# Two cross-attention and expert layers on one core: routing steps of the first attention moved, merged heads put in another PSUM bank

## What is computed

```
x = x + attention0(layernorm(x), ctx, ctx)    # 16 heads of 8 channels, rotary, 256 x 256 scores a head
x = x + experts0(layernorm(x))                # 64 experts, each token's best 8, softmax weights
x = x + attention1(layernorm(x), ctx, ctx)    # one head
x = x + experts1(layernorm(x))                # 16 experts, each token's best 4
```

## Time and profile before

| | us |
|---|---|
| median of three runs | 686.94 (686.65 to 692.87) |
| profiled execution, its own time | 690.62 |
| its span in the profile | 688.9 |
| TensorE busy in the span | 482.5 (70%) |
| VectorE busy | 384.4 (56%) |
| ScalarE busy | 221.6 (32%) |
| GpSimd busy | 349.4 (51%) |

### The profile page before, as it was taken

How to read it: one execution, slowest core, us unless ns; L and a number is a source line. 1 busy time by engine, 2 the same in 40 slices (tenths; PEclk the granted TensorE clock), 3 DMA queues, 4 the chain that set the end, 5 groups by cost and what they waited for, 6 DMA issues and landing times.

```text
span 688.9 us, 12080 instructions
## 1 busy us (share of the span) xinstructions
PE 482.5 (70%) x3519; PEld 368.4 (53%) x3519; DVE 384.4 (56%) x1235; ACT 221.6 (32%) x578; POOL 349.4 (51%) x476
## 2 busy tenths in 40 slices
PE   0741898888898430699989994157764499999960
PEld 0630344444443210688877783145553499999950
DVE  8981576788786460154444442689955044444426
ACT  0451065555667310333323331134431122222210
POOL 9394221115556673256545537014444867777730
PEclk9985599888899655799999998597765599999985
DMA  5089989746588697789999723961111799999927
GB/s 184 4 203 244 341 291 298 218 94 155 166 238 279 208 402 285 229 270 313 347 298 309 244 95 106 353 273 55 70 69 61 258 388 360 349 353 361 375 100 276
DMA packets 82915, 163.95 MB, mean 238 GB/s; under 512 B 13070, under 2 KB 58142, under 8 KB 81072
## 3 DMA queue, kind: packets, MB, share of 16 engines
q1 hardware_dynamic: 56832, 106.20, 46.3%
q0 software_dynamic: 13968, 32.29, 12.7%
q10 hardware_dynamic: 12064, 24.84, 12.4%
HBM read 104.94 MB, written 66.78 MB: 249 GB/s over the span
## 4 chain that ended last, share of the span: by engine, by line
PE 32%; DMA 13%; DVE 9%; issue 2%; POOL 2%; ACT 1%; SPq 1%; POOLq 0%; DVEq 0%
PE sc_ps L1790 11%; DMA hd_side<-held 6%; PE hd_ps_up L1246 6%; PE sc_ps L1772 5%; DMA rows<-hd_side_out,hd_side_target 3%; PE hd_ps_out L1252 2%; DMA sc_rows<-rows 2%; PE hd_ps_x L1224 2%; PE sc_ps L1780 1%; DVE sc_rows L1879 1%; PE sc_ps L1740 1%; POOL rows L1393 1%; PE sc_ps L1728 1%; DVE sc_n_stats L1473 1%; DMA listed<-sc_empty,sc_index 1%
## 5 line engine op out<-in xcount | busy, mean ns | idle before, releaser
L1021 DVE TENSOR_REDUCE at_top<-at_ps_top 128x2 f32<-128x512 f32 x128 | 83.2, 685 | 46.4 <-PE at_ps_top L926 45.6
L1393 POOL DMA_INDIRECT rows<-hd_out,hd_rows x64 | 62.2, 972 | 59.3 <-DVE hd_out L1344 36.9
L1093 ACT ACTIVATE at_prob<-at_ps_score 128x512 f32<-128x512 f32 x128 | 72.6, 594 | 51.2 <-PE at_ps_score L944 50.6
L926 PE MATMUL at_ps_top<-e_arena 96*128 96x256 bf16 x256 | 57.6, 315 | 37.2 <-PEq L107 21.9
L1246 PE MATMUL hd_ps_up<-hd_x_turned,e_arena 128*128 128x160 f32 x512 | 82.7, 305 | 0.0
L1790 PEld LDWEIGHTS sc_ps<-sc_t_turned,e_w 128*112 128x112 f32 x672 | 80.6, 180 | 2.6
L1790 PE MATMUL sc_ps<-sc_t_turned,e_w 128*112 128x128 f32 x672 | 82.0, 276 | 0.0
L1246 PEld LDWEIGHTS hd_ps_up<-hd_x_turned,e_arena 128*128 128x128 f32 x512 | 76.1, 192 | 8.7 <-issue 6.2
L682 POOL DMA_INDIRECT held<-e_extended,e_address x64 | 62.4, 975 | 28.4 <-issue 17.7
L682 POOL DMA_INDIRECT listed<-e_extended,e_address x32 | 33.6, 1049 | 69.0 <-DVE e_address L674 61.5
L1381 DVE TENSOR_TENSOR hd_inner<-hd_silu,hd_ps_up 128x160 f32<-128x160 f32 x64 | 20.5, 321 | 81.8 <-ACT hd_silu L1331 81.8
(11 more groups left out here) (266 smaller groups left out, 911.6 us busy)
## 6 DMA issues: line engine op xcount, KB each, us to landing
e_w<-in_weights SPq DMA_DIRECT2D x42, 704.0 KB, 6.0
e_arena<-in_weights SPq DMA_DIRECT2D x52, 384.0 KB, 11.4
held<-e_empty ACTq DMA_DIRECT2D x16, 960.0 KB, 7.2
hd_rows<-held SPq DMA_DIRECT2D x15, 768.0 KB, 10.5
sc_rows<-rows SPq DMA_DIRECT2D x8, 1024.0 KB, 13.8
sc_tile_rows<-listed SPq DMA_DIRECT2D x42, 144.0 KB
parts<-op_parts SPq DMA_DIRECT2D x8, 576.0 KB, 6.7
e_arena<-in_weights ACTq DMA_DIRECT2D x12, 384.0 KB, 4.0
```

Source lines behind the costliest of these rows:

```text
L926: last = nc.tensor.matmul(ps_top[at % TOPS][:, half, :], q_in[n][0:TOP, columns(at, half)], k_in[n][0:TOP, columns(at)], start=True, stop= ...
L1021: nc.vector.reduce_max(top[:, 2 * h:2 * h + 2], ps_top[at % TOPS][:], AX_X).then_inc(top_found, 1)
L1093: nc.scalar.activation(prob[at % RING][:], ps_score[at % SCORES][:], ACT.Exp, scale=scale).then_inc(prob_ready, 1)
L1393: nc.gpsimd.indirect_dma_start(rows_out, to, out_ap, None, bounds_check=TOKENS * LAYER0.chosen - 1, oob_is_err=False).then_inc(semaphore, 16)
```

## The change

It renumbers the routing steps, gives each batch's eight scatters steps of their own, splits the table of the last two batches, moves the turn, the copy and the placing of the cut maxima one step later each, and puts the merged heads into the second half of the bank of `ps_rows`, with the waits that go with it.

```
-    LOAD, SHARE = 26, 34
-    AMID = dict(load=LOAD, share=SHARE, merge=37, add=38, scale=39, norm=42, turn=46, keep=47, score=51, choose=52, expo=55, rank=55,
-                places=57, targets=59, weights=62, scatter=62)
-    LAST_BUT_TWO = dict(AMID, turn=45, keep=46, score=49, choose=49, expo=50, targets=50, rank=50, places=51, weights=51, scatter=53)
-    LAST_TWO = dict(load=LOAD, share=SHARE, merge=35, add=36, scale=37, norm=37, turn=39, keep=39, score=41, choose=41, expo=42, targets=42,
-                    rank=43, places=43, weights=43, scatter=46)
+    AMID = dict(load=26, share=34, merge=37, add=38, scale=39, norm=42, turn=45, keep=46, score=49, choose=50, expo=52, rank=53,
+                places=54, targets=55, weights=57)
+    LAST_BUT_TWO = dict(AMID, score=48, choose=48, expo=49, rank=49, places=50, targets=50, weights=51)
+    LAST_BUT_ONE = dict(load=26, share=31, merge=32, add=33, scale=34, norm=34, turn=36, keep=36, score=38, choose=38, expo=39, targets=39,
+                        rank=40, places=40, weights=40)
+    LAST = dict(load=26, share=34, merge=35, add=36, scale=37, norm=37, turn=39, keep=39, score=41, choose=41, expo=42, targets=42,
+                rank=43, places=43, weights=43)
+    SCATTERS = (57, 58, 60, 61, 62, 64, 65, 66)
+    LAST_SCATTERS = tuple(range(51, 59))
 
     def __init__(self):
-        of_batch = [self.AMID] * (B - 3) + [self.LAST_BUT_TWO] + [self.LAST_TWO] * 2
+        of_batch = [self.AMID] * (B - 3) + [self.LAST_BUT_TWO, self.LAST_BUT_ONE, self.LAST]
...
+            for k, offset in enumerate(self.SCATTERS if b < B - 3 else self.LAST_SCATTERS):
+                self.scatters.setdefault(b * H + offset, []).append((b, k))
...
-            first = b * H + offsets["scatter"]
-            apart = H // 2 if first < B * H - H - 4 else LAYER0.chosen // 2
-            for k in range(LAYER0.chosen):
-                self.scatters.setdefault(first + k % 4 + k // 4 * apart, []).append((b, k))
...
-        ps_rows = s.psum("ps_rows", [P, P])
+        ps_rows_merged = s.psum("ps_rows_merged", [P, 2 * D])
+        ps_rows, ps_merged = ps_rows_merged[:, 0:P], ps_rows_merged[:, D:]
         ps_merge = s.psum("ps_merge", [P, 2 * D])
-        ps_merged = ps_merge[:, 0:D]
...
-                hh, late = divmod(at + LEAD - 5, HALF)
+                hh, late = divmod(at + LEAD - 6, HALF)
                 if late == HALF - 1 and 0 <= hh < HALVES:
                     place(hh)
...
                 if hh >= 1:
                     pe.wait_ge(rows_kept, hh)
+                if hh == 1:
+                    pe.wait_ge(lift_known, 1)
+                if hh >= 6 and hh % 2 == 0:
+                    pe.wait_ge(x_ready, hh // 2 - 2)
...
                 pe.wait_ge(inputs.loaded, 48)
+                pe.wait_ge(rows_kept, 1)
...
             def merge(b):
-                if b >= B - 2:
-                    pe.wait_ge(routing.rank_read, b)
-                elif b >= 1:
-                    pe.wait_ge(routing.logits_read, b)
-                else:
-                    pe.wait_ge(lift_known, 1)
+                pe.wait_ge(rows_kept, min(2 * b + 6, HALVES))
+                if b >= 1:
+                    pe.wait_ge(x_ready, b)
                 pe.wait_ge(divided, b + 1)
...
-                hh, late = divmod(at + LEAD - 4, HALF)
+                hh, late = divmod(at + LEAD - 5, HALF)
                 if late == HALF - 1 and 0 <= hh < HALVES:
                     turn_tops(hh)
...
-                    if b + 1 < B - 2:
-                        pe.wait_ge(x_ready, b + 2)
                     routing.pe_rank(pe, b)
...
-                hh, late = divmod(at + LEAD - 5, HALF)
+                hh, late = divmod(at + LEAD - 6, HALF)
                 if late == HALF - 1 and 0 <= hh < HALVES:
                     keep_rows(hh)
```

More of the change, by code:

```diff
@@ L752 @@
 class RoutingSteps:
-    LOAD, SHARE = 26, 34
-    AMID = dict(load=LOAD, share=SHARE, merge=37, add=38, scale=39, norm=42, turn=46, keep=47, score=51, choose=52, expo=55, rank=55,
-                places=57, targets=59, weights=62, scatter=62)
-    LAST_BUT_TWO = dict(AMID, turn=45, keep=46, score=49, choose=49, expo=50, targets=50, rank=50, places=51, weights=51, scatter=53)
-    LAST_TWO = dict(load=LOAD, share=SHARE, merge=35, add=36, scale=37, norm=37, turn=39, keep=39, score=41, choose=41, expo=42, targets=42,
-                    rank=43, places=43, weights=43, scatter=46)
+    AMID = dict(load=26, share=34, merge=37, add=38, scale=39, norm=42, turn=45, keep=46, score=49, choose=50, expo=52, rank=53,
[7 more added lines that the diff above has]
+    LAST_SCATTERS = tuple(range(51, 59))
     def __init__(self):
-        of_batch = [self.AMID] * (B - 3) + [self.LAST_BUT_TWO] + [self.LAST_TWO] * 2
-        self.batch = {}
+        of_batch = [self.AMID] * (B - 3) + [self.LAST_BUT_TWO, self.LAST_BUT_ONE, self.LAST]
+        self.batch, self.scatters = {}, {}
         for b, offsets in enumerate(of_batch):
@@ L768, in __init__ @@
                 self.batch[stage, b * H + offset] = b
+            for k, offset in enumerate(self.SCATTERS if b < B - 3 else self.LAST_SCATTERS):
+                self.scatters.setdefault(b * H + offset, []).append((b, k))
         self.end = max(at for _, at in self.batch) + 1
-        self.scatters = {}
-        for b, offsets in enumerate(of_batch):
-            first = b * H + offsets["scatter"]
-            apart = H // 2 if first < B * H - H - 4 else LAYER0.chosen // 2
-            for k in range(LAYER0.chosen):
-                self.scatters.setdefault(first + k % 4 + k // 4 * apart, []).append((b, k))
         self.first_scatter = min(self.scatters)
```

## The result

The changed kernel takes 707.55 us (median of 4, 706.42 to 712.17) where the kernel before takes 686.88 in the same session: ratio 1.0292, 95% interval 1.022 to 1.0364. It is slower by 20.7 us; forecast was 9. The profiled execution took 708.05 us, span 706.3.

What follows compares the result with a forecast made beforehand. The prediction took POOL's end of the first layer's routing, its last 32 scatters, as the bound. Heads 9.1 us later less 0.2 in the tail gave about +9 on the median 686.94: 696.0 us, range 684 to 702.

Steps and rivals of the forecast that it cites:

- The stretch at full clock: Steps from 50, 66, 82, 98: share and choose in one DVE block, 2.4 us per stretch, 2.2 in the last.
- the moved routing score: Routing score's four PE matmuls move from step 16b+35 to 16b+33, where PE is full: 0.5 us per stretch.
- The credit for old half clock: Three earlier stretches: 0.5 us off each, since old half clock there might not be lost twice.
- The first 50 steps: New PSUM bank's waits taken as 0, also at step 40; bounds -0.5 to +0.5 us per batch.
- The clock behind step 50: Batches 0 to 3's closer steps: heads 9.1 us later, without added half clock in the main forecast.
- clock rival: Longer PE stalls behind each share add some 10 us of half clock, 4 us lost, 700 us; chance 0.15.
- The cut behind two scatters: Last stretch, batch 3: two scatters on POOL delay the cut of the last eight heads by 1.2 us.
- The tail: After the heads: batch 4's scatters start 3.6 us earlier, late batch 5 takes back 3.4; 0.2 us won.
- The rival in which POOL decides: Heads don't slip, POOL's scatters run without pause before batch 5: 3.4 us won, 683.5 us; chance 0.15.
- The sum: Whole kernel: +9.1 us for the heads, -0.2 for the tail, about +9.
- 0.45 x 0.85 + 0.15: Chance of a slowdown beyond about 1% (6.9 us), given as about 0.54.
- its formula for the end of the attention stage: Attention's end equals the start of POOL's last unbroken scatter run plus 32 x 1.263 us.

Runs made afterwards that it cites:

- e9: The changed kernel with useless matmuls in all three PE stalls of batches 1 to 4; 700.44 us against 688.77, ratio 1.02.
- e12: The kernel before with batch 4's routing earlier, batch 7's share ten steps earlier, and useless matmuls where PE stands; 684.37 us, ratio 0.9944.
- e2: The changed kernel with the old steps and scatters for batches 0 to 3 alone; 693.03 us against 689.43, ratio 1.0064.
- e10: The kernel before with close steps for batch 4 alone and batch 7's share ten steps earlier; 688.44 us, ratio 1.0003.
- e3: The kernel before with only the turn, copy and placing of the cut maxima one step later; 690.1 us, ratio 1.0014.
- e1: The changed kernel with all routing steps and scatters put back to the old, keeping the shared bank, its waits and the shift; 692.4 us, ratio 1.004.
- e11: The kernel before with useless matmuls behind each share and scale and in step 21; 686.17 us, ratio 0.9959.
- e8: The changed kernel with 28 useless matmuls in the PE stall behind each share of batches 1 to 4; 710.6 us, ratio 1.029.
- e7: The changed kernel with the first two scatters of batches 0 to 4 moved behind the cut of the maxima; 707.68 us, ratio 1.0278.

## Why the prediction was half right

**The stretch at full clock (right).** By hand the new order cost 1.9 us per stretch and 0.5 for the moved routing score, 2.4, and 2.2 in the last: 9.4 for four. e9 and e12 have the two orders with no half clock at all between steps 50 and 107: 20.2, 20.0, 20.1, 13.5 us against 17.8, 18.2, 17.8, 12.0. That is 2.4, 1.8, 2.3 and 1.5, sum 8.0. The filling doesn't blur this on the old side: e2's unfilled first and third stretches, at full clock, take 17.8 us too. The details came as worked out too: PE stands 2.74 (2.95 said), DVE pauses 1.02 (0.95), step 70 starts 5.93 us into the stretch (6.0).

**The credit for old half clock (sign right, too large).** I took off 1.5 us. Half clock costs 72.0 - 65.8 = 6.2 us between steps 50 and 107 in the kernel before and 79.3 - 73.8 = 5.5 in after: 0.7 off. So this piece grew by 7.3, for which 7.9 was forecast. That agreement is luck. The credit was read off one execution that had much half clock; measured from e10, which runs the old code, the piece grew by 11.4, and measured from e2 by 12.5.

**The first 50 steps (the first step that failed).** The prediction took the new PSUM bank as 0 by its waits in the stretches and at step 40, and did not price what comes with it: turn, keep and place one step later, and the product for the lift ahead of the second turn. PE waits 2.8 us longer for placed rows (e3 shows that the shift does it) and 0.94 us for the lift at 88.15. The timeline of PE after:

```profile
86.18 0.61 PE L947 MATMUL at_ps_score<-e_arena 99*128 99x256 bf16 x2 [1.79 <-DMA e_arena<-at_top_rows]
88.15 0.38 PE L937 MATMUL at_ps_rows_merged<-identity,at_top_parts 128*48 128x128 f32 x1 [0.94 <-DVE at_lift L1043]
```

These steps, up to step 50, run at half clock for 18.3 us, where it was 10.0, and take 5.9 us more (e1 with the old steps: 6.1). The forecast had 0. What this costs in the end is less sure: e1, which has it with the old steps, is slower by 2.8 us (0.6 to 4.9).

**The clock behind step 50 (the second step that failed).** The prediction gave the closer steps of batches 0 to 3 no half clock of their own; it took 1.5 us off for old half clock and left the rest to a rival at 0.15. It had 9.1 us for these steps (3 x 2.4 + 3.4 - 1.5). e2 and after differ in them and their scatters alone, and lie 2.3% apart, nearly 16 us. In their profiles the piece from step 50 to 107 is 79.3 - 66.8 = 12.5 us longer; 8.0 is the order itself, and the other 4.5 is what 13.5 us more of half clock cost, a third of it. The new order has three stalls behind every share and keeps 17.0 us of half clock. That is the clock rival's mechanism. Its price doesn't follow from its own terms (four times 6 less two times 3 is 18, not 10), so that its 4 us lost come near is luck.

The clock isn't the whole of the miss. With the idle places filled in both orders and no half clock left between steps 50 and 107, e9 and e11 still stand 2.4% apart (1.02 and 0.9959), where after and before stand 2.9% apart. Of these 16.6 us the order is 8.0 and the end 1.5 by their profiles; I put the remaining 7 down to the front and the start (argued, not tried alone). e1 puts the front at 2.8, and the intervals are too wide to choose. How much half clock the old order has behind a later front stays open too (16.9 and 6.8 us in two executions of the same code).

The Trainium skill, "TensorE: Matmul & The Clock Gate", section "Part 1: The HAM clock gate", says that low is the default state and idleness brings it back. The traces agree: 12.4 us more of PE's waiting for maxima, rows and lift (8.7 + 2.8 + 0.9) go with 13.3 us more of half clock (40.2 against 26.9 in the table), and matmuls in all the idle places between steps 50 and 107 take all of it out there. e8 doesn't fit as well: PE's waiting for maxima falls from 21.8 to 17.1 us and the half clock doesn't fall (44.4 us for 43.6, from 84 us on).

**The cut behind two scatters (seen, worth nothing).** The cut starts at 226.64, 1.1 us behind the last maximum's end, as said (1.2). In e7 the cut follows the last maximum at once, and nothing is gained. The piece behind step 107 grew by 2.5 us, with 4.9 us of half clock in it; e9, with the same scatters and no half clock, has 18.0 us, so 1.7 is left for everything else there.

**The tail (right).** 0.2 us won by forecast, 0.4 measured; batch 5 late and the pause ahead of it near 3 us. The rival in which POOL decides fell by the pause it named.

**The sum.** 8.0 for the order, -0.7 of credit, 5.9 for the front, 1.3 for the start, 2.5 for the end: 17.0 of the 17.1 us in the profile. It adds up because the pieces are cuts of the same two profiles, and proves no cause. Two slips in the prediction change nothing: 0.45 x 0.85 + 0.15 is 0.53, and its formula for the end of the attention stage leaves out the 8 us from the last scatter to the first row load. The medians stand 20.7 apart, the profiled pair 17.4, since the profiled execution of the kernel before was 3.7 us above its median.

## What to carry to other kernels

Where two engines run in order with two buffers between them, the size of one block matters more than how much work there is: 1.1 us of choice moved next to 2.1 us of share, with places and targets moved behind add and scale, cost some 2 us a stretch without an instruction added. In this kernel an idle place of PE cost twice, once itself and then through the clock, at about a third of a microsecond (0.32 to 0.37) for each one at half clock, PE sharing the path with DVE; so price each moved helper by the PE stall that it makes, from the first step on. And where executions of one kernel differ by 4 us in one piece, take a price from several of them. A gain behind such a stretch (3.6 us on POOL) must be weighed with that.

## What the runs showed of the hardware that was not expected

The longest stall isn't needed for the clock to fall: e8, with the 2.74 us stall cut to 1.17 and those of 1.1 to 1.5 us left, stays at 0.86 over the heads; e9, with these filled too, has 0.94, and e12 0.99. The same code had 16.9 us of half clock in one execution and 6.8 in another. Work that nobody needs shortened the unchanged kernel: 0.9959 (0.993 to 0.9989) with 220 matmuls more over the heads.
